# A four-layer graph network on one core: layer 3's attention weights are also written to a PSUM bank, and VectorE multiplies the gathered rows from there

## What is computed

```
h = (x @ W).reshape(N, 4, 32);  a_src = sum(h * att_src);  a_dst = sum(h * att_dst)
logits = leaky_relu(a_src[src] + a_dst[dst], 0.2)
e      = exp(logits - seg_max[dst])              # one weight per edge and head
out    = segment_sum(h[src] * e / segment_sum(e), dst) + bias
out    = relu(layernorm(out) * gamma + beta)
```

## Time and profile before

| | before |
|---|---|
| median of 3 runs | 5992.94 us (5991.13 to 5996.12) |
| profiled execution | 5991.14 us |
| its span in the profile | 5986.0 us |
| busy over the span | PE 4755.2, PEld 3820.7, DVE 2700.2, ACT 2011.3, POOL 3180.1 us |
| gathers of layer 3 on POOL | from 3879.2 to 5949.2 us, 1612 instructions |

### The profile page before, as it was taken

One profiled execution on the slowest core, in us unless ns is written; L12 is line 12 of the kernel. 1 busy time (PEld: TensorE's weight loads), 2 busy tenths in 40 slices (PEclk: granted clock), 3 DMA queues, 4 the chain that ended last, 5 costly groups with the idle time before them and its releaser, 6 DMA issues.

```text
span 5986.0 us, 76959 instructions
## 1 busy us (share of the span) xinstructions
PE 4755.2 (79%) x25981; PEld 3820.7 (64%) x25981; DVE 2700.2 (45%) x10045; ACT 2011.3 (34%) x4004; POOL 3180.1 (53%) x3344
## 2 busy tenths in 40 slices
PE   6999999899999999999998999835454454445454
PEld 5888888667777777777777999834443444444443
DVE  8888888333333333333334444334343343434344
ACT  5777777322222222222223555411111111111111
POOL 1000000477777777777770000077777777777775
PEclk9999999999999999999998999966777777777777
DMA  6666666677776766676664777522222222222221
GB/s 145 149 142 144 144 145 145 183 208 210 206 209 205 209 203 206 202 206 203 205 203 127 237 234 234 177 54 55 55 54 54 55 55 54 55 55 54 55 55 43
DMA packets 479268, 842.71 MB, mean 141 GB/s; under 512 B 73876, under 2 KB 301764, under 8 KB 467364
## 3 DMA queue, kind: packets, MB, share of 16 engines
q0 software_dynamic: 141920, 462.69, 30.8%
q1 hardware_dynamic: 322852, 365.35, 19.7%
q10 hardware_dynamic: 14112, 9.74, 0.5%
HBM read 682.31 MB, written 155.18 MB: 140 GB/s over the span
## 4 chain that ended last, share of the span: by engine, by line
PE 61%; POOL 20%; issue 8%; DVE 5%; ACT 2%; DMA 2%; ACTq 0%; DVEq 0%; POOLq 0%
POOL ring L509 20%; PE bank L970 17%; PE bank L957 11%; PE bank L1136 9%; PE bank L657 6%; PE bank L641 3%; PE bank L555 3%; DMA ring<-htab,src 2%; PE bank L1446 1%; PE bank L1410 1%; ACT at L621 1%; PE bank L1439 1%; DVE hs L603 1%; PE bank L896 1%; DVE hs L601 1%
## 5 line engine op out<-in xcount | busy, mean ns | idle before, releaser
L509 POOL DMA_INDIRECT ring<-htab,src x1612 | 1579.0, 980 | 504.7 <-issue 471.2
L509 POOL DMA_INDIRECT ring<-ptab,src x1612 | 1525.0, 946 | 539.9 <-issue 446.6
L970 PE MATMUL bank<-ring,oh 128*126 128x384 f32 x3224 | 1219.0, 489 | 0.0
L926 DVE TENSOR_TENSOR ring<-bank,ring 128x512 f32<-128x512 f32 x806 | 552.6, 691 | 1397.1 <-PE bank L957 1133.0
L957 PE MATMUL bank<-w1e,ea 128*128 128x256 f32 x3224 | 832.2, 381 | 16.1 <-DVE ring L926 9.1
L621 ACT ACTIVATE at<-bank 128x343 fp32r<-128x343 f32 x1612 | 753.9, 488 | 255.2 <-PE bank L641 218.1
L940 ACT ACTIVATE ring<-ring 128x1024 f32<-128x1024 f32 x403 | 425.5, 1056 | 1228.6 <-DVE ring L926 1228.6
L657 PE MATMUL bank<-xhl,at 128*126 128x258 f32 x4410 | 831.6, 325 | 4.0 <-ACT at L621 0.2
L957 PEld LDWEIGHTS bank<-w1e,ea 128*128 128x128 f32 x3224 | 612.7, 191 | 279.8 <-DVE ring L926 21.0
L1402 PE MATMUL bank<-ident,pk 128*72 128x128 f32 x90 | 38.4, 426 | 877.5 <-ACT pk L1364 877.5
L970 PEld LDWEIGHTS bank<-ring,oh 128*126 128x126 f32 x3224 | 590.4, 188 | 218.7 <-issue 0.6
(11 more groups left out here) (256 smaller groups left out, 5366.5 us busy)
## 6 DMA issues: line engine op xcount, KB each, us to landing
atab<-at POOLq DMA_DIRECT2D x90, 1543.5 KB, 9.6
ring<-ea_r SPq DMA_DIRECT2D x403, 256.0 KB, 4.0
ea<-ea_t SPq DMA_DIRECT2D x403, 256.0 KB, 3.1
adjb<-atab SPq DMA_DIRECT2D x180, 535.5 KB, 4.6
adjb<-atab SPq DMA_DIRECT2D x90, 472.5 KB, 4.0
ring<-ptab,src POOLq DMA_INDIRECT x1612, 3.4
ring<-htab,src POOLq DMA_INDIRECT x1612, 2.5
ptab<-pO ACTq DMA_DIRECT2D x49, 128.0 KB, 3.8
```

The source lines that it names most:

```text
L509: return e.indirect_dma_start(o, None, table, bass.IndirectOffsetOnAxis(ap=src[:, t:t + 1], axis=0))
L926: e.tensor_tensor(group1(gi, m % 2), MLP[m % 3][:, :].rearrange("p (g f) -> p g f", g=2), group1(gi, m % 2), ALU.add).then_inc(s_edge, 1)
L970: e.matmul(SUM[s % 2][0:SL, 0:384], slots_of(s, i), rv1[:, t // G % NR1, t % G, :], start=i == 0, stop=t == END[s]).then_inc(s_sum1, 1)
```

## The change

The exponentials of a step are computed twice by ACT: first into bank 6 of PSUM (`weights3`, 72 columns), then, as before, into `ring`, where PE needs them for the sum of the weights. DVE's multiplication takes its second operand from bank 6. `s_exp` therefore counts two per step, and ACT waits, before it overwrites bank 6, until all six multiplications of every earlier step are done. The output of L1417 moves from bank 6 to columns 256 and up of bank 4. The sum that PE makes and the in-place result in `ring` are as before.

```diff
+            def weights3(o, n):
+                return bank[6][:, 0:4 * GT].rearrange("p (t h) -> p t h", h=4)[:, o:o + n, :]
...
                 elif k == 13:
...
                     if s:
-                        e.wait_ge(s_exp, s)
+                        e.wait_ge(s_exp, 2 * s)
...
-                            e.wait_ge(s_exp, g + 1)
-                            e.tensor_tensor(m, m, rv3[:, o:o + n, 128:132].unsqueeze(3).broadcast_to([P, n, 4, 32]),
+                            e.wait_ge(s_exp, 2 * g + 2)
+                            e.tensor_tensor(m, m, weights3(k, n).unsqueeze(3).broadcast_to([P, n, 4, 32]),
                                             ALU.mult).then_inc(s_weigh, 1)
...
-                            e.activation(o2T[:, 0:nb, :], bank[6][:, 0:nb * SL].rearrange("p (b q) -> p b q", b=nb),
+                            e.activation(o2T[:, 0:nb, :], bank[4][:, 2 * P:2 * P + nb * SL].rearrange("p (b q) -> p b q", b=nb),
...
                             e.wait_ge(s_logit, LOG3 * f + 3)
+                            if f:
+                                e.wait_ge(s_weigh, -(-GT // CH) * f)
+                            e.activation(weights3(0, tiles(f)), zl[:, 0:tiles(f), :], ACT.Exp, bias=0.0,
+                                         scale=1.0).then_inc(s_exp, 1)
                             e.activation(rows3(f, tiles(f))[:, :, 128:132], zl[:, 0:tiles(f), :], ACT.Exp, bias=0.0,
                                          scale=1.0).then_inc(s_exp, 1)
...
-                                m = e.matmul(bank[6][:, i * SL:(i + 1) * SL], oh2[0:SL, f % 4, i * P:(i + 1) * P],
+                                m = e.matmul(bank[4][:, 2 * P + i * SL:2 * P + (i + 1) * SL], oh2[0:SL, f % 4, i * P:(i + 1) * P],
```

## The result

| | before | after |
|---|---|---|
| median, 4 runs each | 5992.03 us (5985.29 to 5996.12) | 5934.60 us (5933.51 to 5943.72) |
| ratio, with 95% interval | | 0.9907 [0.9893, 0.9921] |
| profiled execution, its span | 5991.14, 5986.0 us | 5943.72, 5941.8 us |
| layer 3: first gather, last gather | 3879.2, 5948.2 us | 3884.9, 5899.9 us |
| from the last gather's end to the end of the span | 36.8 us | 41.0 us |

The change makes the kernel faster by 0.93%, by the medians 57 us, where 5943 us were forecast and 5933 to 5956 us given as the range. In some of the later series, each on one chip with the kernel before beside the others, every kernel took some 600 to 700 us more; their times are compared only within the series.

A forecast was written before the change was run, and what follows sets the result against it. Layer 3 was taken as bound by POOL's gather pitch plus a tail: 58 us of lengthening removed, 9 us of residue back, 0.6 us of tail added, -48.4 us, forecast 5943 us, range 5933 to 5956 us.

The forecast's parts named there:

- POOL's pitch is the layer: Layer 3: its time is the number of gathers times the start-to-start pitch, mean 1.2843 us, plus a tail.
- 58 us lie in gathers behind DVE instructions, and L1341 holds them: Layer 3: gathers starting during the two-SBUF-input multiplication stand until it ends; one PSUM input removes all 58 us.
- The prediction's check: 183 gathers beginning inside an L1341 hold 38.8 us; its end minus gather start minus 0.12 us sums to 42.5.
- The residue of 9 us: Layer 3: lengthening left from other DVE instructions without a PSUM input, from evenly spread gather starts; 9 us, ends 0 and 18.
- The multiplication keeps its duration: Layer 3, DVE: L1341 stays at 0.55 us with a PSUM input; cost 0 in the middle whichever it is.
- One more activation, ACT's wait, the move to bank 4: no cost in the middle: Layer 3: 24 us more ACT work and a loop 0.5 to 0.6 us longer per step, covered by ACT's idle 9.7 us.
- The tail, 0.6 us: After the last gather: a multiplication waits for the last step's two activations, adding 0.6 us, ends 0 and 1.5.
- The sum: Whole kernel: -58 + 9 + 0.6 = -48.4 us, from 5991.14 to 5942.7 us, forecast as 5943 us.
- The lock that stays: Rival, layer 3: the lock ignores the second input's place, or input order matters; no gain, 5993 us, chance 0.06.
- the large residue: Rival, layer 3: unpushed gathers meet other DVE instructions in most steps, 27 us instead of 9; 5961 us, chance 0.07.
- the longer multiplication: Rival, layer 3: L1341 still blocks and gets longer reading PSUM, 21 us more at 0.62 us; 6012 us, chance 0.03.
- The consumers as the bound: Rival, layer 3: ACT's wait or slow multiplications exceed 9.7 us per step; 180 us on top at 2.5 us each; next to nothing.

The follow-up runs named there:

- The compact SBUF copy: Changed kernel with the second copy of the weights in its own SBUF buffer instead of PSUM bank 6: 6598.84 us against 6589.11 for the kernel before.
- the operand alone: Changed kernel, but the multiplication reads its weights from the ring in SBUF again: third run 5984.26 us against 5985.73 for the kernel before, 0.9996.
- after_again: The changed kernel run again with nothing altered, beside the kernel before: 6631.52 us against 6589.11, 1.0065.

## Why the prediction was right, step by step

*POOL's pitch is the layer.* Right in the first measurement, and in every profile from a series with the kernel before at 5990 us: no wait for the ring above 0.3 us. Layer 1, whose gathers nothing touches, kept its 2048 us (2048.3 before, 2047.9 after), as it had to.

*58 us lie in gathers behind DVE instructions, and L1341 holds them.* Right. The compact SBUF copy and the operand alone bring the long gathers back, PSUM in either place removes them. The runs show means of 1.12 to 1.16 us for gathers inside a multiplication with two SBUF inputs and 0.94 to 0.95 us with one. The prediction's check, 38.8 us held where the formula gives 42.5, was better than it looked: from each instruction's own times 182 gathers hold 37.7 us and the formula gives 37.4 (about 42 only where multiplications in a row count as one). What it didn't take apart is a second kind: 23 gathers like that of the earlier trace rows take 1.60 us each, 15 of the 57 us. Each began inside L1283, 0.02 to 0.04 us before an L1341 that L1280 follows, while 14 gathers that began just as shortly before other L1341 took 0.94 to 0.95 us. With the operand alone in the ring there are 17 of them again; in the changed kernel there is none, though there only 4 gathers begin inside the same scaling (now L1287) where before 24 did, and these take 0.94 to 0.97 us. Why this row of three holds a gather that began ahead of the multiplication, no run shows. The rule of the Trainium skill that I had weighed (SBUF — State Buffer, section "Who interferes with whom") agrees with both.

*The residue of 9 us.* Too large. The gathers hold 1525.0 - 1612 x 0.944 = 3.3 us over the normal duration. The even spread that I took for the starts is not what happens: the steps repeat, and the meetings with other two-input instructions are few and end early (14 gathers of 1.045 us or more, none above 1.087). The 54.0 us instead of 49 are mainly this term. The 8 us that the moved timing is worth by itself were not in the sum; in the changed kernel they can't be added, since there is nothing left to avoid.

*The multiplication keeps its duration.* Right: 543 ns against 546. The Trainium skill (VectorE: DVE Perf Modes, section "The TRN2 errata — SBUF-src ops pay a fixed extra latency per instruction") gives a PSUM source a larger fixed cost per instruction than an SBUF source; this trace does not show it for one PSUM input beside one in SBUF.

*One more activation, ACT's wait, the move to bank 4: no cost in the middle.* Right in outcome. The loop grew by more than I had worked out, because I overlooked the table load, which stands in front of the exponential in 48 of 90 steps: behind it the first multiplication of the next step waits up to 1.8 us, 54.6 us in all in the waits shown above, where it waited for nothing before. Over the whole layer 33 of 36 such waits come with a load (61.6 us in all); with the exponential into the ring first, 36 waits are 10.9 us. ACT's 8.6 us of standing for rows cover it.

*The tail, 0.6 us.* Inside its ends of 0 and 1.5, by a step it didn't have: 1.1 us, with the table load. The 3.1 us of PE's last branch are in the span and not in the time.

*The sum.* Forecast -49 + 0.6 = -48.4 us; layer 3 gave -54.0 + 1.1 = -52.9 us. The mis-sized term is the residue. The median came 8 us lower than forecast: 4.5 of them are this; the rest isn't accounted for by layer 3 and lies within the interval. Layer 3 alone would have given 5991.1 - 52.9 = 5938 us. The other 3 to 4 us, which no term explains, left the median 1.6 us above the lower end of the range, so that it still held is in part luck.

*The rivals.* The lock that stays, the large residue and the longer multiplication are all excluded by the profile after. The consumers as the bound, which I gave next to nothing, is what the long series show for the changed kernel, though for a reason that no row of mine held.

## What to carry to other kernels

When GpSimd issues indirect DMAs back to back and sets the time, look for VectorE instructions with two SBUF inputs that run as a gather starts. Count the gathers' time over their median, and move one operand of the longest such instruction to PSUM: a small copy by ScalarE was enough here. It pays only while the gathers set the time: in the long series the changed kernel was 0.15 to 0.65% slower than the kernel before. A second wait in front of an activation that needs a table load can push the load behind that wait; give the load an activation with an earlier wait to follow.

## What the runs showed that was not expected

In four of the seven series behind the first measurement (on chips 12, 15, 10 and 11) the kernel before took 6589 to 6622 us, in three (chips 11, 0 and 3) 5986 to 5991; chip 11 showed both. In the profiled executions of the long ones the time is in the two layers with gathers. The kernel before has no profile from one of them. The changed kernel's second profile (`after_again`) has its layer 1 gathers from 1111.8 to 3463.6 us, 2352 us instead of 2048, and its layer 3 gathers from 4184.5 to 6542.2 us, 2358 instead of 2015 ("remote" is the profile's word for a releaser that it can't name):

```profile
L509 POOL DMA_INDIRECT ring<-htab,src x1612: 942/947/1085, 4184.5 to 6542.2; - x180
...
  issue: 454.1, 1469
  PE bank L1454: 219.4, 80
  remote: 156.2, 62
```

What a step looks like there (timeline, layer 3):

```profile
4618.18 1.15 PE L1418 MATMUL bank<-rT,sel 72*126 72x128 f32 x8 [2.27 <-ACT rT L1377]
...
4627.25 0.95 POOL L509 DMA_INDIRECT ring<-htab,src  x1 [0.30 <-issue]
...
4631.05 0.69 DVE L1200 TENSOR_TENSOR tops<-bank,away 126x512 f32<-126x512 f32 x1 [12.63 <-remote]
4631.11 0.38 ACT L1383 ACTIVATE o2T<-bank 128x252 f32<-128x252 f32 x1 [12.98 <-remote]
4631.49 0.95 POOL L509 DMA_INDIRECT ring<-htab,src  x1 [3.29 <-remote]
4631.54 1.01 PE L1433 MATMUL bank<-hs,o2T 128*126 128x4 f32 x4 [10.39 <-ACT o2T L1383]
```

DVE and ACT start 11 to 12 us after PE's matmuls for them have ended by the profile, within 0.1 us of each other, and some 3 us after POOL's last gather ended; POOL had stopped for a full ring. PE itself gets ACT's update within 0.1 us. In the first measurement L1200 started 0.04 us after the last matmul of L1418 in all 90 steps; here it is 7.5 us at the median. A pause of POOL isn't what ends the wait each time: of the 74 steps in which L1200 starts more than 1 us late, it starts more than 1.5 us behind a gather's end in 46, and beside running gathers in 28; with the operand in the ring (its second run) in 12 and 61 of 73. TensorE's granted clock was a little lower as well (0.65 against 0.71 between 4200 and 5800 us), which can be a consequence as well as a cause. The profiles of these series also hold only some 19 thousand records of DMA landings where the others hold 73 thousand, so that a wait may lack its releaser in them. What makes PE's results late, and why a series has it or not, these runs don't show. Under it short gathers bought nothing, and PSUM as the operand's place was 27 us slower than SBUF in one series (6631.52 against 6604.33) and 6 us faster in another (6635.91 against 6641.75).
